# Key layout in a fused attention and expert kernel: the four parts of a key innermost, in place of four separate rows

## The reference, cut to what matters

```
def attention(x, y):                               # x: 8 x 256 x 256, y: 8 x 77 x 192
    q = (x @ wq + bq).reshape(B, Sq, H, D)         # H = 16 heads, D = 16
    k = (y @ wk + bk).reshape(B, -1, H, D)
    v = (y @ wv + bv).reshape(B, -1, H, D)
    scores = einsum('bhqd,bhkd->bhqk', q, k) / sqrt(D)
    out = einsum('bhqk,bhkd->bhqd', softmax(scores), v)
    return out.reshape(B, Sq, E) @ wo + bo
x = x + tanh(g_xattn) * attention(layernorm(x), ctx_768)
xf = layernorm(x)                                  # 2048 tokens
top1 = argmax(softmax(xf @ gate_w.T))
routed = relu(xf @ w1[top1] + b1[top1]) @ w2[top1] + b2[top1]
shared = relu(xf @ sw1 + sb1) @ sw2 + sb2
x = x + tanh(g_ffn) * (routed + shared)
```

## Time and profile before

| what | value |
|---|---|
| median of 3 runs | 333.23 us (333.08 to 334.18) |
| the profiled execution: time, span | 334.0 us, 332.2 us |
| granted TensorE clock, mean | 0.998 |
| PE busy | 317.3 us (96%) |
| PE weight loads (PEld) busy | 281.9 us (85%) |
| DVE, ACT, POOL busy | 229.9, 214.7, 177.5 us (69%, 65%, 53%) |
| mean DMA rate | 107 GB/s |
| DMA packets; under 512 bytes | 38151; 16608 |

### The profile page before, as it was taken

How to read it: one execution, slowest core, us unless ns; L and a number is a source line. 1 busy time by engine, 2 the same in 40 slices (tenths; PEclk the granted TensorE clock), 3 DMA queues, 4 the chain that set the end, 5 groups by cost and what they waited for, 6 DMA issues and landing times.

```text
span 332.2 us, 7324 instructions
## 1 busy us (share of the span) xinstructions
PE 317.3 (96%) x2383; PEld 281.9 (85%) x2383; DVE 229.9 (69%) x517; ACT 214.7 (65%) x483; POOL 177.5 (53%) x261
## 2 busy tenths in 40 slices
PE   7998889999999999999999999989899999999993
PEld 7776767779887878887988889979899999999992
DVE  6899989997697997896537649943445455454473
ACT  3757999679958655879493865536547555564652
POOL 6266997835755086449340577512536535544552
PEclk9999999999999999999999999999999999999999
DMA  7877844731017044101006501444524511222200
GB/s 196 271 239 207 224 95 105 214 94 13 3 16 216 2 104 118 67 13 66 0 2 201 180 32 63 151 123 175 190 98 155 205 47 65 80 63 66 78 32 28
DMA packets 38151, 35.69 MB, mean 107 GB/s; under 512 B 16608, under 2 KB 35060, under 8 KB 37613
## 3 DMA queue, kind: packets, MB, share of 16 engines
q1 hardware_dynamic: 34568, 27.36, 28.1%
q0 software_dynamic: 2720, 7.32, 6.8%
q10 hardware_dynamic: 837, 0.67, 0.7%
HBM read 21.20 MB, written 9.85 MB: 93 GB/s over the span
## 4 chain that ended last, share of the span: by engine, by line
PE 60%; issue 11%; POOL 7%; DMA 7%; DVE 6%; SPq 4%; ACT 3%; POOLq 1%; ACTq 0%; DVEq 0%
PE y_ps L1545 20%; PE h_ps L1545 14%; PE s_ps L1545 10%; PE bank L1545 9%; PE bank L1678 4%; POOL sorted_dram L710 2%; DMA stage<-in_ctx 2%; DMA sorted_dram<-empty_rows 2%; SPq L482 1%; POOL hT_lo L719 1%; DVE smax L1249 1%; DMA part_dram<-x_all 1%; PE bank L1782 1%; DVE rsum L1267 1%; DMA part<-part_dram,gather_token 1%
## 5 line engine op out<-in xcount | busy, mean ns | idle before, releaser
L693 POOL TENSOR_TENSOR probs<-probs,rinv 128x616 f32<-128x616 f32 x32 | 40.8, 1287 | 34.4 <-DVE rinv L1271 34.4
L1545 PE MATMUL y_ps<-sw,hT_hi 128*128 128x256 f32 x272 | 57.8, 292 | 1.1 <-DVE hT_lo L1523 0.7
L1545 PE MATMUL y_ps<-ew,hT_hi 128*128 128x256 f32 x256 | 54.4, 287 | 1.1 <-DVE hT_lo L1482 1.1
L1482 DVE TENSOR_TENSOR hT_lo<-h,hT_hi 128x256 fp32r<-128x256 f32 x64 | 30.1, 471 | 35.6 <-ACT h L1089 33.8
L1545 PEld LDWEIGHTS y_ps<-sw,hT_hi 128*128 128x128 f32 x272 | 44.9, 190 | 2.5 <-DVE hT_lo L1523 1.7
L1545 PEld LDWEIGHTS y_ps<-ew,hT_hi 128*128 128x128 f32 x256 | 42.6, 188 | 2.4 <-DVE hT_lo L1482 2.4
L1545 PE MATMUL h_ps<-x2T_hi,sw 128*128 128x512 f32 (+1 forms) x160 | 44.0, 362 | 0.0
L1086 ACT ACTIVATE hT_hi<-h_ps,vec_cols 128x256 fp32r<-128x256 f32 x32 | 15.2, 475 | 39.6 <-PE h_ps L1545 32.6
L1545 PE MATMUL y_ps<-sw,hT_lo 128*128 128x256 f32 x136 | 38.3, 282 | 0.0
L1545 PE MATMUL y_ps<-ew,hT_lo 128*128 128x256 f32 x128 | 35.9, 280 | 0.0
L959 ACT ACTIVATE pT<-bank 128x512 f32<-128x512 f32 x40 | 24.2, 623 | 16.3 <-PE bank L1678 16.2
(11 more groups left out here) (208 smaller groups left out, 826.8 us busy)
## 6 DMA issues: line engine op xcount, KB each, us to landing
v_diag<-v_rows SPq DMA_DIRECT2D x16, 256.0 KB
stage<-in_L_ffn_w SPq DMA_DIRECT2D x4, 1024.0 KB, 6.1
sw<-ew SPq DMA_DIRECT2D x4, 1024.0 KB
xs<-sorted_dram SPq DMA_DIRECT2D x8, 257.0 KB, 2.7
stage<-in_L_ffn_sw SPq DMA_DIRECT2D x2, 1024.0 KB, 6.8
x_all<-in_x SPq DMA_DIRECT2D x1, 1536.0 KB, 8.4
part_dram<-x_all SPq DMA_DIRECT2D x3, 512.0 KB, 5.1
k_dram<-probs SPq DMA_DIRECT2D x2, 616.0 KB, 5.4
```

Of the source, the lines that this page charges most:

```text
L693: nc.gpsimd.tensor_tensor(pq, pq, rinv[:, b % 2, k, :].unsqueeze(2).to_broadcast([P, HG, KEYS]), ALU.mult).then_inc(p_ready, 1)
L1482: nc.vector.tensor_tensor(hT[1][:, c % HB, 0:RTOK], h32[:, c % 2, 0:RTOK], hT[0][:, c % HB, 0:RTOK], ALU.subtract).then_inc(h_lo, 1)
L1545: return nc.tensor.matmul(out_, lhsT, rhs, start=start, stop=stop, **kw)
```

## The change

The four parts of a key become the innermost dimension everywhere: in `k_parts` on chip, in `k_dram` in memory and in `k_own` on chip. ScalarE and GpSimd write `k_parts` with a step of four elements (16 bytes); GpSimd also reads the high part with that step. The store of a half moves one run of 4,928 bytes for a partition in place of four of 1,232. A load of one head moves 1,232 bytes for a partition in one run in place of four runs of 308 bytes. The moving operand of the score matmuls is read with a step of four elements. `k32` is read and written in order as before. The number of instructions of each kind and the orders stay as they are.

```
-    k_dram = nc.dram_tensor("k_dram", (P, 2 * GROUPS, BATCHES * KEYS), F32).ap()
+    k_dram = nc.dram_tensor("k_dram", (P, BATCHES, KEYS * 2 * GROUPS), F32).ap()
-        k_own = sb("k_own", [P, 2, 2 * GROUPS, HH, KEYS], F32R, scope=att)
+        k_own = sb("k_own", [P, 2, HH, KEYS, 2 * GROUPS], F32R, scope=att)
-        k_parts = probs[:, 1, :, :].rearrange("p q n -> p (q n)").rearrange("p (m g n) -> p m g n", m=2, g=GROUPS)
+        k_parts = probs[:, 1, :, :].rearrange("p q n -> p (q n)").rearrange(
+            "p (b k c) -> p b k c", b=BATCHES, k=KEYS)
# keys_out (SP)
-                sp.dma_start(k_dram[:, :, cols], k_parts[:, :, :, cols].rearrange("p m g n -> p (m g) n")
-                             ).then_inc(k_out[half], 16)
+                sp.dma_start(k_dram[:, batches, :].rearrange("p b n -> p (b n)"),
+                             k_parts[:, batches, :, :].rearrange("p b k c -> p (b k c)")).then_inc(k_out[half], 16)
# keys_in (SP), for each of 8 heads
-                    sp.dma_start(k_own[rows, n, :, h % HH, :].bitcast(F32), k_dram[rows, :, b * KEYS:(b + 1) * KEYS]
+                    sp.dma_start(k_own[rows, n, h % HH, :, :].rearrange("p k c -> p (k c)").bitcast(F32), k_dram[rows, b, :]
                                  ).then_inc(k_in[n], 16)
# keys_lo (POOL)
-                nc.gpsimd.tensor_tensor(k_parts[:, 1, g, cols].bitcast(F32R), k32[:, g, cols], k_parts[:, 0, g, cols],
-                                        ALU.subtract).then_inc(k_lo, 1)
+                nc.gpsimd.tensor_tensor(k_parts[:, batches, :, GROUPS + g].bitcast(F32R), k32[:, g, batches, :],
+                                        k_parts[:, batches, :, g], ALU.subtract).then_inc(k_lo, 1)
# keys (ACT)
-                to = k_parts[:, 0, g, cols].bitcast(F32R) if rounded else k32[:, g, cols]
-                nc.scalar.activation(to, key_bank(half, g), ACT.Copy).then_inc(k_hi if rounded else k_32, 1)
+                to = k_parts[:, batches, :, g].bitcast(F32R) if rounded else k32[:, g, batches, :]
+                nc.scalar.activation(to, key_bank(half, g).rearrange("p (b k) -> p b k", k=KEYS), ACT.Copy).then_inc(k_hi if rounded else k_32, 1)
# scores (PE)
-                                     k_own[rows, b % 2, km * GROUPS + g, :, :].rearrange("p h k -> p (h k)"), n == 0, n == 2)
+                                     k_own[rows, b % 2, :, :, km * GROUPS + g].rearrange("p h k -> p (h k)"), n == 0, n == 2)
```

More of the change, by code:

```diff
@@ L284, in build @@
         k32 = xn2[:, :, :, :].rearrange("p a t r -> p (a t r)")[:, 0:GROUPS * GK].rearrange(
-            "p (g n) -> p g n", g=GROUPS)
-        k_parts = probs[:, 1, :, :].rearrange("p q n -> p (q n)").rearrange("p (m g n) -> p m g n", m=2, g=GROUPS)
+            "p (g b k) -> p g b k", g=GROUPS, k=KEYS)
+        k_parts = probs[:, 1, :, :].rearrange("p q n -> p (q n)").rearrange(
+            "p (b k c) -> p b k c", b=BATCHES, k=KEYS)
         b2_rows = h32[:, 0, 0:EXPERTS * DIM]
@@ L467, in keys_out @@
                 sp.wait_ge(k_lo, GROUPS * (half + 1))
-                cols = slice(half * YH, (half + 1) * YH)
-                sp.dma_start(k_dram[:, :, cols], k_parts[:, :, :, cols].rearrange("p m g n -> p (m g) n")
-                             ).then_inc(k_out[half], 16)
+                batches = slice(half * BATCHES // 2, (half + 1) * BATCHES // 2)
+                sp.dma_start(k_dram[:, batches, :].rearrange("p b n -> p (b n)"),
+                             k_parts[:, batches, :, :].rearrange("p b k c -> p (b k c)")).then_inc(k_out[half], 16)
             def keys_in(b):
```

## The result

The changed kernel takes 342.31 us (median of 4 runs, 342.10 to 345.79), the kernel before 333.53 us in the same comparison (333.08 to 334.18): ratio 1.0286, 95% interval 1.0218 to 1.0354. The prediction said 340.0 us, slower, range 331.8 to 350. The profiled execution took 342.3 us with a span of 340.5; the one before 334.0 and 332.2, so 8.3 us are to be accounted for.

What follows compares the result with a forecast made beforehand. TensorE was taken to bound the kernel from 70 us on, DVE, ACT and POOL from 31 to 70. 334.0 + 5.8 + 1.4 - 0.4 = 340.8 us profiled, 340.0 us in the metric, range 331.8 to 350.

Steps and rivals of the forecast that it cites:

- What bounds the kernel: TensorE from 70 us on; DVE, ACT and POOL from 31 to 70 us; the key-loading chain before.
- Late quarters: The 16 quarters of score matmuls behind 70 us: 0.36 us more each, fully visible, +5.8 us.
- The pace of a stepped stream: Score matmuls on TensorE: strided keys stream at half pace, +0.12 us a pair, +0.36 us a quarter.
- the nearest row: Batch 0's plain float32 matmuls on TensorE, 0.26 us per 308-column record, taken as the pace for strided keys.
- the stagger and the last transition: Weight loads around a quarter's score matmuls on TensorE, claimed to stay as they were because their operand is unchanged.
- Early quarters: The 12 quarters before 70 us: about five lack slack; a third of the 4.3 us bound shows, +1.4 us.
- Writing the keys: Strided writes on the path: +0.1 us per ACT step, +0.2 per POOL step, +0.6 us until the store is issued.
- Loads: SP's eight issues for batch 1's keys: -1.0 us; with slower writes, keys land 0.4 us earlier, -0.4 us.
- The sum: Whole kernel: 334.0 + 5.8 + 1.4 - 0.4 = 340.8 us for the profiled execution, 340.0 us in the metric.
- A: Rival: the step costs TensorE nothing and the loads win at the start, 332.0 us; chance 0.12.
- B: Rival: step free on TensorE, but ACT and POOL writes eat the gain or issues don't shorten, 333.2 us; chance 0.08.
- C: Rival: TensorE pays for the whole spread, four times the present stream, about 363 us; chance 0.12.

Runs made afterwards that it cites:

- run with late quarters only: Kernel before, with the step of 4 in the score matmuls of batches 4 to 7 alone (wrong keys there): 339.64 us, ratio 1.0202.
- step 2: Changed kernel with only the two groups interleaved, so that engines step by 2 elements (8 bytes): 342.03 us, ratio 1.026.
- runs of 4: Kernel before, twelve late quarters each reading another key pattern, one of them 4 neighbours then a gap of 12: 334.26 us, that pattern 0.14 us a pair.
- runs without a step: Changed kernel with the parts as four rows of 77, 333.48 us; and changed kernel with score matmuls reading 308 neighbouring elements (wrong keys), 333.78 us.
- run without steps: Changed kernel with a head's four parts as four rows of 77 in one run of 1,232 bytes, no engine stepping: 333.48 us, ratio 1.002.
- early run: Kernel before, with the step of 4 in the score matmuls of batches 1 to 3 alone (wrong keys there): 338.16 us, ratio 1.0142.
- the step alone: Kernel before, each score matmul reading its keys with a step of 4 elements (wrong keys), run twice: 344.59 us and 342.57 us.
- step 8: Kernel before, each score matmul reading 154 elements 32 bytes apart, twice (wrong keys): 342.94 us, ratio 1.0269.
- run with pairs: Kernel before, each score matmul reading 154 pairs of neighbours, the pairs 32 bytes apart (wrong keys): 342.85 us, ratio 1.0266.

## Why the prediction was right, and where its sizes were off

- What bounds the kernel: right behind 70 us. Late quarters 16 x 0.39 = 6.2 us against 5.8 forecast. In the run with late quarters only the last quarter starts 6.1 us late, and the span shows 5.8.
- The pace of a stepped stream: half, as taken from the nearest row, 0.28 us a pair against 0.26. That a step goes at the pace of plain float32 was in part luck, for no row tied the two. I also held the stagger and the last transition fixed; they grew from 0.25 to 0.35 and from 0.23 to 0.39 us. The reason I gave, that every fetch of a new place costs TensorE a turn, was too coarse: step 2 shares places between elements and costs as much, runs of 4 jump 77 times and cost nothing.
- Early quarters: the term that was mis-sized. I took 1.4 us, a third of 12 x 0.36; the thirteenth quarter starts 2.9 us late in the changed kernel, and 3.1 us are lost between the first quarter and it, two thirds of 12 x 0.39. I weighed a score's slack against DVE alone, quarter by quarter. But what stands behind a score on TensorE's list, the turns and projections that ACT and DVE wait for, moves as well, and the lateness adds up. The chain of waits of the changed kernel shows it (start us, us, what): from 45.55 us on every score is on the path, with the turns and projections between them. Of the twelve early quarters eleven are in it, where before's chain has four and I had counted five:

```profile
45.55 1.10 PE s_ps L1546 x6
...
50.40 1.01 PE s_ps L1546 x6
51.41 1.62 PE bank L1546 x12
53.03 0.44 PE bank L1679 x4
53.47 1.01 PE s_ps L1546 x6
...
57.97 1.08 PE s_ps L1546 x6
59.05 0.59 PE bank L1618 x4
59.64 2.94 PE bank L1546 x20
62.58 0.44 PE bank L1679 x4
63.01 1.01 PE s_ps L1546 x6
```

- Writing the keys: POOL +0.17 us an instruction against +0.2, right; the ratio of the Trainium skill's page (GPSIMD Engine Reference, Performance pitfalls for Q7 kernels), half as long again, is not what a subtraction of 308 columns does here: 1.014 / 0.842 = 1.20. ACT +0.325 us against +0.1, mis-sized: I reasoned that a slow engine does not feel the step. The store is issued 0.80 us later, +0.6 forecast, and the delay is not handed on as I had it: SP's first load of the keys starts 0.20 us late (24.72 against 24.52).
- Loads: a single issue 0.420 us against 0.443 forecast, right, but the eight for batch 1 together not. They were to take 1.0 us less and took 0.38 less:

```profile
24.52 5.18 SPq L482 DMA_DIRECT2D k_own<-k_dram  x8
24.72 4.80 SPq L483 DMA_DIRECT2D k_own<-k_dram  x8
```

  The last one starts no earlier than before. What comes in earlier is the landing: 1.8 us in the median of all loads against 2.2. The first score came 0.13 us earlier against 0.4: I followed ACT's writes only to the store, and not to what stands behind them on ACT's list: batch 1's normalised inputs start at 16.16 us in place of 15.68, batch 0's scores came 0.47 us late, and they took the place of the wait removed. The run without steps, in which ACT writes at 0.434 us, has these scores at 26.86 us, where before had 26.80.
- The sum: 340.8 us forecast for the profiled execution, 342.3 measured. Too little by 0.4 late and by 1.9 up to the thirteenth quarter (start included, +1.0 forecast); 0.9 of that is hidden, since the 334.0 us that I started from held slow routed experts. Between the medians, 342.3 against 340.0, the whole 2.3 us show. Of the rivals, A and B are excluded by the runs without a step, C by the 0.28 us.

## What to carry to other kernels

Before parts are interleaved to get longer transfers, price the engine that reads them: 28 quarters took 0.39 us more of TensorE each, of which 8.8 us showed, for issues that were 0.17 us shorter and mostly off the path. The same length of run comes for nothing if each part stays a row inside the run. And before the start of one thing in two traces is compared, compare the granted clock up to it: 1.65 of the early run's 4.8 us were the clock. A delay on one engine's list is to be followed through everything behind it there, not only to the engine that waits for the delayed result.

## What the runs showed of the hardware that I had not expected

- A float32r moving operand of TensorE at 2.4 GHz keeps its full pace only while at least four columns come from each 16 bytes (77 pieces for 308 columns, 0.14 us); with two or one it takes 0.26 to 0.28 us, at all distances tried, 8 to 32 bytes. One element repeated is free (0.14).
- Plain float32, at 0.26 us for a record of 308 columns, takes 0.27 with a step of two.
- ACT's write of 308 elements takes 0.431 us unbroken, 0.460 with a step of 8 bytes, 0.756 with one of 16; POOL's subtraction 0.842 (0.784 in rows of 77), 0.860 and 1.014 us.
- In one execution the matmuls from 6.5 to 11.4 us ran at half pace, though the granted clock reads 1.00 there, and all that followed stayed 2.1 us late.
- In four of the seven profiled executions with stepped early quarters (the step alone twice, step 8, the early run), and in none of the six others, the granted clock fell to 0.50 a few us behind the first quarter, for 3.1 to 3.4 us and at a cost of 1.4 to 1.7 us. TensorE had been busy since that quarter began, and had waited 1.2 to 1.4 us for the keys before it. The run with pairs shows the same wait and the same work without a fall, so what decides it is open. Whether this is also why unprofiled executions of one kernel lie up to 4 us above its lowest time isn't shown.
